# Moving the first batch's row maxima and query casts out of the latent attention block

## The reference

```
q_big  = (x_norm @ Wq.T) per head @ w_kc_q          # layer 2 also ropes q_big
k      = rope(ctx)                                   # 1500 keys x 64
q_r    = q_big @ W_qr ; k_r = k @ W_kr               # folded: q = q_r W_kr^T, 16 heads x 56 rows x 64
scores = q @ k.T                                     # 896 query rows x 1500 keys
attn   = softmax(scores)                             # needs a maximum for every query row
out    = ((attn @ k) @ w_kc_kv) @ Wo.T
```

## Time and profile before

| what | value |
|---|---|
| median of three runs | 1624.45 us |
| the profiled execution | 1626.06 us, of it 1624.3 us span |
| mean granted TensorE clock, share of full | 0.977 |
| queries_plain, from the end of top8_ffn's work to the attention block | 118.0 to 163.9 us |
| first exact scores of layer 1, of layer 2 | 184.36 us, 872.22 us |
| one batch of latent attention afterwards | about 26.2 us |

### The profile page before, as it was taken

The page is one execution under the profiler, slowest core; times in us unless marked ns, Lnnn a source line. Parts: engine busy times, 40 slices in busy tenths (PEclk is TensorE's granted clock), DMA queues, the critical chain, the costliest instruction groups (busy, mean ns, idle before and its releaser), DMA issues. The chain is left out here.

```text
span 1624.3 us, 39337 instructions
## 1 busy us (share of the span) xinstructions
PE 1530.7 (94%) x17028; PEld 1221.2 (75%) x17040; DVE 891.4 (55%) x1624; ACT 649.1 (40%) x931; POOL 667.8 (41%) x482
## 2 busy tenths in 40 slices
PE   6899899999999999888998999999999999898998
PEld 3475688888888877676656888888888778646465
DVE  3950566766666536775546655555565253377112
ACT  3544344454444442652013444444444332144221
POOL 5415664465445200543966643664451030170101
PEclk9999899999999999999998999999999999999999
DMA  8006565654563202315025646545541030152402
GB/s 239 2 16 144 113 154 134 136 123 105 117 152 74 68 20 85 105 49 131 0 58 115 157 107 138 114 97 118 133 91 28 21 101 1 50 199 75 149 24 62
DMA packets 66460, 154.45 MB, mean 95 GB/s; under 512 B 14972, under 2 KB 44220, under 8 KB 65424
## 3 DMA queue, kind: packets, MB, share of 16 engines
q1 hardware_dynamic: 65520, 150.10, 36.8%
q0 software_dynamic: 768, 1.84, 0.4%
HBM read 87.51 MB, written 5.51 MB: 57 GB/s over the span
## 5 line engine op out<-in xcount | busy, mean ns | idle before, releaser
L1624 DVE TENSOR_REDUCE latent_psW<-latent_psW 128x1 f32<-128x500 f32 x654 | 418.4, 682 | 233.0 <-PE latent_psW L1519 232.6
L1602 ACT ACTIVATE latent_w<-latent_psS 125x896 f32<-125x896 f32 x384 | 351.9, 920 | 427.8 <-PE latent_psS L1537 424.2
L1547 PEld LDWEIGHTS latent_psO<-latent_val,latent_w 125*64 125x64 f32 x10752 | 323.9, 138 | 25.2 <-issue 11.6
L1547 PE MATMUL latent_psO<-latent_val,latent_w 125*64 125x65 f32 x10752 | 339.6, 223 | 0.4 <-issue 0.4
L1536 PE MATMUL latent_psS<-latent_qA,latent_kA 128*125 128x448 f32 x768 | 290.1, 378 | 3.9 <-DVE latent_qB L1640 2.3
L1537 PE MATMUL latent_psS<-latent_qB,latent_kB 128*125 128x448 f32 x768 | 282.6, 368 | 0.0
L1519 PE MATMUL latent_psW<-latent_kA,latent_qA 128*128 128x500 f32 x654 | 213.8, 396 | 3.4 <-DMA latent_qA<-latent_qh 1.7
L1536 PEld LDWEIGHTS latent_psS<-latent_qA,latent_kA 128*125 128x125 f32 x768 | 143.4, 187 | 31.1 <-ACT latent_w L1602 4.6
L1537 PEld LDWEIGHTS latent_psS<-latent_qB,latent_kB 128*125 128x125 f32 x768 | 143.6, 187 | 19.7
L1519 PEld LDWEIGHTS latent_psW<-latent_kA,latent_qA 128*128 128x128 f32 x654 | 123.9, 190 | 20.7 <-DVE latent_psW L1624 5.9
L946 POOL TENSOR_TENSOR latent_rawT<-latent_rawT,latent_ropeT 128x1000 f32<-128x1000 f32 x48 | 110.8, 2336 | 34.0 <-DMA latent_rawT<-in_ctx_cols 22.2
(11 more groups left out here) (403 smaller groups left out, 2146.5 us busy)
## 6 DMA issues: line engine op xcount, KB each, us to landing
latent_qA<-latent_qh SPq DMA_DIRECT2D x128, 112.0 KB, 2.5
latent_rawT<-in_ctx_cols SPq DMA_DIRECT2D x32, 375.0 KB, 5.8
latent_rawT<-in_ctx_cols SPq DMA_DIRECT2D x64, 187.5 KB, 6.4
latent_raw<-in_ctx SPq DMA_DIRECT2D x32, 375.0 KB
latent_kA<-latent_high SPq DMA_DIRECT2D x32, 375.0 KB, 3.9
latent_kB<-latent_high SPq DMA_DIRECT2D x32, 375.0 KB, 5.3
latent_kA<-latent_rawT SPq DMA_DIRECT2D x32, 375.0 KB, 6.2
experts_wgu<-in_L_gu SPq DMA_DIRECT2D x8, 1024.0 KB, 16.5
```

The costliest lines, as they stand in the source:

```text
L1547: last = pe.matmul(sums[r:r + 64, c, :], w[t % ROUND][:, queries_of(c, r):queries_of(c, r) + 64], val[b % 2][:, t, :], start=(t == 0 and c ...
L1602: act.activation(w[t % ROUND][:, :].rearrange("p (h n) -> p h n", h=2), psS[0:KP, t % 2, :, 0:GH], ACT.Exp).then_inc(exp_done, 1)
L1624: dve.tensor_reduce(bank[:, THIRD + j:THIRD + j + 1], bank[:, 0:THIRD], mybir.AxisListType.X, ALU.max).then_inc(max_ready, 1)
```

## The change

- Layer 1, loads. `LatentFirst` is made before `top8_ffn`, and SP issues the first pair's columns, tables and rows in that stage instead of in `queries_plain`.
- Layer 1, order. POOL ropes the keys before it fills the constants. `high_keys` stands ahead of the query copies on ACT. The queries are computed h outermost, so that batch 0 is complete after the eighth unit; then ACT casts its high part, POOL makes its low part, and SP stores qA and qB of batch 0 in this stage.
- Layer 1, maxima. The 21 maxima matmuls of batch 0 stand behind query units 10 to 15 (three each behind 10, 11, 12, four each behind 13, 14, 15), in six PSUM banks; DVE writes the partial maxima to SBUF.
- Layer 2. ACT casts the queries of batch 0 before the last group of query copies, POOL empties qB and subtracts the low part, and SP stores both in `queries_roped`. The maxima stay where they were.
- Both. At the start of `latent_attention` SP issues the mask first, then qA of batch 1, then the columns of batches 2 and 3. `keep_busy` has 6 calls instead of 18. POOL clears less. The mask has a buffer of its own.

```diff
-def top8_ffn(nc, g, weights, later):
+def top8_ffn(nc, g, weights, later, first):
+            @block.sync
+            def _(sp):
+                first.load(sp)
...
+    def empty_queries(self, pool, norm):
+        pool.wait_ge(norm.turned_ready, NT)
+        pool.memset(self.mx[:, :, :], 0.0).then_inc(self.empty, 1)
+        pool.wait_ge(self.empty, 1)
+        pool.memset(self.qB[64:128, :].bitcast(F32), 0.0).then_inc(self.empty, 1)
+        pool.wait_ge(self.empty, 2)
+    def high_queries(self, act, q):
+        act.copy(self.qh[:, :].rearrange("p (j s) -> p j s", s=S), q[:, :, 0:S]).then_inc(self.qh_ready, 1)
+    def low_queries(self, pool, q):
+        pool.wait_ge(self.qh_ready, 1)
+        pool.tensor_tensor(self.ql[:, :].rearrange("p (j s) -> p j s", s=S), q[:, :, 0:S],
+                           self.qh[:, :].bitcast(F32).rearrange("p (j s) -> p j s", s=S), ALU.subtract).then_inc(self.ql_ready, 1)
+    def store_queries(self, sp):
+        GH = HP * S
+        self.store(sp)
+        sp.wait_ge(self.qh_ready, 1)
+        for e in range(2):
+            for r in range(2):
+                sp.dma_start(self.qA[r * 64:r * 64 + 64, e * GH:(e + 1) * GH].bitcast(F32),
+                             self.qh[e * 64:e * 64 + 64, :].bitcast(F32)).then_inc(self.qA_came[0], 16)
+        sp.wait_ge(self.ql_ready, 1)
+        for e in range(2):
+            sp.dma_start(self.qB[0:64, e * GH:(e + 1) * GH].bitcast(F32),
+                         self.ql[e * 64:e * 64 + 64, :].bitcast(F32)).then_inc(self.qB_came[0], 16)
...
 queries_plain
+        max_bank = lambda x: (norm.turned, ps_z, ps_y)[x % 6 // 2][:, x % 2, 0:first.THIRD]
-                first.load(sp)
-                first.store(sp)
+                first.store_queries(sp)
...
+                first.rope_keys(pool, 0)
                 first.fill(pool)
-                first.rope_keys(pool, 0)
                 first.rope_rows(pool, 0)
                 first.low_keys(pool, 0)
+                first.empty_queries(pool, norm)
+                first.low_queries(pool, q)
...
+                def score_for_max(x):
+                    j, m = x // 3, x % 3
+                    wait_from(pe, first.max_ready, x - 5)
+                    pe.matmul(max_bank(x), first.qA[:, j * 128:(j + 1) * 128], first.kA[0][:, first.part(m)],
+                              start=True, stop=True).then_inc(first.max_scores, 1)
+                x = 0
+                for n in range(2 * HP):
+                    queries(n)
+                    if n == 2 * HP - 6:
+                        pe.wait_ge(f["taken"], HP)
+                        pe.wait_ge(first.kA_came[0], 48)
+                        pe.wait_ge(first.qA_came[0], 64)
+                    for _ in range(max(0, n - 2 * HP + 7) and (3 if n < 2 * HP - 3 else 4)):
+                        score_for_max(x)
+                        x += 1
...
+                first.high_keys(act, 0)
                 for n in range(2 * HP):
-                    j, h = n // 2, n % 2
+                    h, j = n // HP, n % HP
...
-                    if n == 3:
-                        first.high_keys(act, 0)
+                    if n == HP - 1:
+                        act.wait_ge(q_taken, HP)
+                        first.high_queries(act, q)
...
+                for x in range(MAX):
+                    dve.wait_ge(first.max_scores, x + 1)
+                    dve.tensor_reduce(parts[:, x % 3, x // 3:x // 3 + 1], max_bank(x), X, ALU.max).then_inc(first.max_ready, 1)
+                dve.wait_ge(first.max_ready, MAX)
+                dve.wait_ge(first.empty, 2)
+                dve.tensor_reduce(first.mx[:, 0, 0:QTL], parts[:, :, :].rearrange("p m j -> p j m"), X, ALU.max).then_inc(first.maxima_ready, 1)
...
 queries_roped
+                    if group == 2 * QUADS - 2:
+                        act.wait_ge(q_taken, 2 * group + 2)
+                        first.high_queries(act, q)
...
+                    if n == 18:
+                        first.empty_queries(pool, norm)
+                first.low_queries(pool, q)
...
 latent_attention
-                store_queries(0)
+                sp.dma_start(mask[:, :, :], d["max_mask"].rearrange("p (c n) -> p c n", n=128)).then_inc(mask_came, 16)
                 store_queries(1)
-                sp.dma_start(mask[:, :, :], d["max_mask"].rearrange("p (c n) -> p c n", n=128)).then_inc(mask_came, 16)
-                store_low_queries(0)
                 n.load_columns(sp, 2)
                 n.load_columns(sp, 3)
...
-                keep_busy(pe, g, psO[:, 0:128], 18)
-                pe.wait_ge(cleared, 6)
-                for x in range(NX):
-                    score_for_max(0, x, alone=True)
+                keep_busy(pe, g, psO[:, 0:128], 6)
+                if not n.maxima_made:
+                    for x in range(NX):
+                        score_for_max(0, x, alone=True)
                 turn_maxima(0)
...
-                high_queries(0)
                 high_queries(1)
```

More of the change, by code:

```diff
@@ L876, in __init__ @@
         self.rawT_came = [a.sem(f"rawT_came{u}") for u in range(2)]
+        self.qA_came = [a.sem(f"qA_came{u}") for u in range(3)]
+        self.qB_came = [a.sem(f"qB_came{u}") for u in range(2)]
+        self.qh_ready, self.ql_ready, self.max_scores, self.max_ready, self.maxima_ready, self.empty = (
+            a.sem(n) for n in ("qh_ready", "ql_ready", "max_scores", "max_ready", "maxima_ready", "empty"))
+        self.nc, self.g, self.layer, self.maxima_made = nc, g, layer, False
         self.kA_came = [a.sem(f"kA_came{u}") for u in range(3)]
@@ L1126, in _, with queries @@
                 pe.wait_ge(rest.a_ready, HP // 2)
-                n = 0
-                for j in range(HP):
-                    for h in range(2):
-                        if n >= 2:
-                            pe.wait_ge(q_taken, n - 1)
-                        for c in range(CC):
-                            last = pe.matmul(ps_q[:, n % 2, 0:HALF], aw[:, j, c, :, :], g.xnT[:, c, h * HALF:(h + 1) * HALF],
-                                             start=(c == 0), stop=(c == CC - 1))
-                        last.then_inc(q_done, 1)
-                        n += 1
+                def queries(n):
+                    h, j = n // HP, n % HP
+                    if n >= 2:
+                        pe.wait_ge(q_taken, n - 1)
+                    for c in range(CC):
+                        last = pe.matmul(ps_q[:, n % 2, 0:HALF], aw[:, j, c, :, :], g.xnT[:, c, h * HALF:(h + 1) * HALF],
+                                         start=(c == 0), stop=(c == CC - 1))
+                    last.then_inc(q_done, 1)
+                def score_for_max(x):
[13 more added lines that the diff above has]
+                        x += 1
             @block.scalar
@@ L1239, in queries_roped @@
         ctx.callback(w.kept.close)
+        first.place_queries()
+        first.place_loads()
         first.place()
@@ L1657, in _ @@
                     dve.memset(lanes[0][:, 0:1], 0.0).then_inc(lanes_summed, 1)
-                dve.wait_ge(cleared, 6)
-                for x in range(NX):
-                    maximum(0, x, alone=True)
-                maxima(0, alone=True)
+                dve.wait_ge(n.empty, 2)
+                if not n.maxima_made:
+                    for x in range(NX):
+                        maximum(0, x, alone=True)
+                    maxima(0, alone=True)
                 take_maxima(0)
@@ L1736, in _, with latent_layer @@
                 norm.vector_tile(dve, NT - 1)
-def latent_layer(nc, g, d, layer, queries, weights, following, magnitudes=None):
-    first = LatentFirst(nc, g, d, layer)
+def latent_layer(nc, g, d, layer, queries, weights, following, first, magnitudes=None):
     queries(nc, g, d, g.q, g.fold, weights, first)
@@ L2636, in program @@
             w = ahead
-            top8_ffn(nc, g, w, later)
+            first = LatentFirst(nc, g, d, 1)
+            first.place_loads()
+            top8_ffn(nc, g, w, later, first)
             w.ctx.close()
-            w = latent_layer(nc, g, d, 1, queries_plain, later, TernaryWeights, magnitudes=g.magnitudes[:, :])
+            w = latent_layer(nc, g, d, 1, queries_plain, later, TernaryWeights, first, magnitudes=g.magnitudes[:, :])
             clear_semaphores(nc)
```

66 lines of the change are left out of this document (44 added, 22 removed).

## The result

The changed kernel takes 1634.51 us, the median of 13 runs (1629.42 to 1636.57), against 1626.44 for 13 runs of the kernel before on the same chip. The ratio is 1.0051, 95% interval 1.0041 to 1.0062: 8.3 us slower (6.7 to 10.1), where no difference was forecast. Its profiled execution took 1635.5 us.

The account below looks back on a forecast made before the run. PE, busy 94% of the span, was taken as the bound, with batch 1 starting when POOL's rope chain allows. Layer 1 +2.8 and layer 2 -3.3 gave -0.5: 1624.0 us beside the median, range 1618.1 to 1627.9.

Parts of the forecast that it names:

- Loads a stage earlier: Ten load issues moved beside `top8_ffn`, where SP has nothing else: cost 0; POOL's ropes begin at about 118 instead of 135.
- rival 3: At the start of `queries_plain` POOL's sums hold up DVE's scalings: up to 3.7 us later, 1627.7 us; chance 0.09.
- the rule that the prediction quotes: POOL and DVE share ports held per instruction; one-input DVE scalings collide only if they run in a two-port mode.
- Queries and maxima in the stage: In `queries_plain`, added query and maxima work makes layer 1's attention block open at 170.4 instead of 163.94, 6.5 us later.
- Start of the block: Layer 1's attention block, without batch 0's casting and maxima: first exact scores at 174.1 instead of 184.36, 10.3 us won.
- The columns: Layer 1's columns of batches 2 and 3 go out 1.9 us later, land in 9.6 (7.6 to 10.4); POOL starts at 183.6.
- T0: The opening of the attention block, forecast at 170.4 in layer 1.
- The two waits: Layer 1: ACT waits for POOL's sums, leaving 4.6 of 10.3 us; PE waits at batch 2's maxima until 214.5, 1.3 later.
- rival 2: Batch 2's qA lands faster, shortening the chain by 5 us; with layer 2 it gains 7.0: 1617.4 us; chance 0.12.
- Clock: Layer 1: PE's idle 4 to 6 us at the start of batch 1 lowers its clock, costing 1.5 us (0 to 2.6).
- Layer 2: Only query work moves; block opens at 853.3, batch 2's maxima come at about 897.6: 3.3 us earlier (2.0 to 4.0).

Follow-up runs that it names:

- only the collision out: Changed kernel with POOL's three rope products kept early, its sums and fills waiting until DVE's eight scalings are done: 1627.11 us, ratio 1.0014.
- with both out: Changed kernel with POOL's sums waiting for DVE's scalings and the low keys of batches 0 and 1 made before batch 0's rows: 1627.43 us, ratio 1.0009.
- The kernel with the columns early: Changed kernel with all roping behind the scalings, plus layer 1's columns of batches 2 and 3 issued in `queries_plain`: 1623.74 us, ratio 0.9990.
- the run with the fills moved: Kernel before the change, with POOL's four constant fills moved beside DVE's eight layer norm scalings: 1627.02 us in one execution.

## Why the prediction was wrong, by its own steps

**POOL beside DVE: the step that failed.** "Loads a stage earlier" was costed at 0, and the collision was rival 3, at 0.09 and at most 3.7 us, "against it: no row shows such a hold-up". For the scalings that was no evidence: before, POOL did nothing beside them, so no row of theirs could show it. For DVE as a whole it was not true. The trace of before has rows further on, in the feed-forward behind layer 1: the same addition (112x512) on DVE alone, and beside a subtraction on POOL.

```profile
664.69 0.69 DVE L1755 TENSOR_TENSOR ffn_h<-ffn_h 112x512 f32<-112x512 f32 x1
...
677.10 1.63 DVE L1755 TENSOR_TENSOR ffn_h<-ffn_h 112x512 f32<-112x512 f32 x1
```
```profile
676.91 1.27 POOL L1756 TENSOR_TENSOR ffn_h<-ffn_h 112x512 f32<-112x512 f32 x1
```

Six of the eight L1755 lie beside a POOL instruction and take 1.24 to 1.64 us, two lie alone and take 0.69. They have two inputs in SBUF and the scalings one, so they do not settle the case, but 0.09 was too little beside them. The other argument, POOL's product beside DVE's maxima, was about DVE reading PSUM. The price was too low as well, because I counted the three sums alone, while the fills and `turn_rows` follow them without a gap: 10.44 - 2.67 = 7.8 us on DVE, of which the stage lost 6.1 (L857 19.7 us after the head, L853 13.6 before). And I asked whether the scalings run in a two-port mode and left it there. Their pace of 0.33 us for 256 columns does not answer it, since L253's statistics of the same 256 columns have it too and were not held up. By the rule that the prediction quotes, the measured hold-up beside memsets does. From the changed kernel to the one without the collision and without the late low keys the change against before goes from +8.3 to +1.5: 6.8 of the 8.8 us that the result lies above the forecast, each known to some 2 us either way.

**Queries and maxima in the stage.** Predicted opening 52.3, measured 52.0 with the collision and the late low part out. But the wait for qA (1.7, bounds 0 to 2.5) was too low for the order of the change itself: 4.28 us with only the collision out. SP begins with qA when it was predicted to, 32.3 us after the head against 32.6, but directly behind the pair's stores, and its four issues take 4.75 us instead of 2.39. The sum had no term for that. In the changed kernel it lay hidden. Taking out one of the two is worth less than both: 2.7 us at the block's opening against 6.3.

**Start of the block.** Right: exact scores 3.7 us behind the opening predicted, 4.4 after, 3.4 with both out.

**The columns.** Issue at T0 + 3.6 predicted, 3.0 measured. Landing 9.6 predicted, 10.8 after and 11.6 in the kernel with both out, above my upper bound of 10.4, which was the slower of two rows. There it puts 1 us on layer 1 (POOL at 66.5 instead of 65.5).

**The two waits.** Right in place, cause and kind. ACT waits 11.34 (12.57 with both out) instead of 9, PE 4.99 (4.11), and the chain from POOL's start takes 31.3 against 30.7 to 31.0. The kernel with the columns early confirms it: both shrink. What rival 2 asked, whether qA of batch 2 lands faster now, the landings answer: its last transfer needs 7.9 us (7.5 before), against 2.3 for the last of batch 1's at the block's start, and PE starts 0.1 after it. The columns of batches 4 and 5 are issued directly behind it. That they slow it is not shown: no run issued them later.

**Clock.** Predicted 1.5 (0 to 2.6). Before and after, the transposes of batch 2's maxima start here:

```profile
234.66 0.28 PE L1524 MATMUL latent_psW<-all_ident,latent_mx 128*32 128x128 f32 x1
```
```profile
243.89 0.28 PE L1616 MATMUL latent_psW<-all_ident,latent_mx 128*32 128x128 f32 x1
```

That is 10.6 later from the stage's head, where batch 2's first maxima matmul was 8.3 later. The difference, 2.3 us, is the low clock behind PE's wait. It lies within the bounds, above the 1.5 taken. With both out it is 1.6 (4.3 later against 2.7).

**Layer 2.** Predicted -3.3 (-2.0 to -4.0). In its own frame (ACT's copies there are 9.5 later than before) the block opens at 853.6 (predicted 853.3), the exact scores at 870.1 (869.6, and 872.22 before) and batch 2's matmul at 898.98 against 901.07: -2.1. PE's old wait is gone but PE runs the first tiles at 0.57 us a matmul until 885, 5.4 us from the first exact scores. Before, the low clock lasted some 3.4 us from there (granted 0.50 from 872.2 to 875.0, 0.90 from 875.0 to 878.0). Half of the 2.0 us between, 1.0, is my estimate of what this cost, most of the 1.2 that are missing; the prediction had a clock term for layer 1 only. The mechanism was right, the size 1.2 too large.

**In sum**: layer 1 is 8.3 later at batch 2 and 2.3 more by the clock, layer 2 gives 2.1 back: +8.5 from the head of the stage, against +8.3 measured. The head came 1.40 us earlier in this execution than in that of before, and about 2 us more are lost behind layer 2's attention; I did not trace either. The head lies at 114.70 to 118.10 in the kernels of the table, and the stretch behind layer 2's attention takes 333.2 to 336.2 us in them (333.8 before, 335.9 after).

## What to carry to other kernels

Before POOL work is moved, list every DVE instruction that it will lie beside, and count all the POOL instructions that follow on, memsets too: each can stand before one DVE instruction. "No row shows it" excludes nothing where the trace of before never had the two together; look for the pair of engines in the rest of the trace. An early start of one engine is worth nothing until the load that ends the next chain starts early too. Here that load and the order of POOL's steps behind it were worth 17 us on top of the moved maxima, and moving the maxima alone, with the collision taken out, nothing that can be measured. How much of the 17 us the early load and the order would give to the kernel before, without the moved maxima, no run tried.

## What the runs showed of the hardware

- While POOL runs, fp32 `tensor_scalar` from SBUF to SBUF on DVE goes at the pace of one per POOL instruction: 8 in 10.44 us beside sums, memsets and products, 6.85 beside four memsets, 4.26 beside the last two of three additions, 2.67 alone. The prediction counted no memset.
- A DVE addition with two inputs in SBUF (L1755 of before, 112x512) takes 0.69 us alone and 1.24 to 1.64 beside a POOL subtraction of 1.27.
- DVE's layer norm statistics (L253) take 2.71 us for eight beside POOL's products, after, beside its memsets, before, and alone, in the run with the fills moved.
- Four issues of qA on SP took 2.39 us when SP came to them after a pause, and 4.75 directly behind four key copies.
- From SP's first issue of the same 1.5 MB to POOL's start it took 10.0 us before and up to 11.6 in these runs.
- The last transfer of qA took 2.3 us from issue to landing at the block's start and 7.9 at batch 1, in the trace of after.
